# Row maxima of causal attention: the mask added by VectorE inside the maximum, and router logits with stationary weights

## What is computed

```
h = layernorm(x) * (1 + ca) + sa                 # ca, sa, ga ... from silu(c) @ wmod
q, k = [content 16 | rope 64] per head, 16 heads # latent queries 192, latent keys/values 64
attn = softmax(q @ k^T * SCALE + causal mask)    # 512 x 512 per head
x = x + ga * (attn @ v) @ w_out.T
h = layernorm(x) * (1 + cb) + sb
probs = softmax(h @ gate_weight.T)               # 32 experts, the router logits
w_tg = top 8 of probs, normalised, summed by group (8 groups)
act = silu(gate) * up                            # 8 experts chosen beforehand, 96 wide
x = x + gb * sum_g w_tg * (act_g @ down_g)
```

## Time and profile before

| | us |
|---|---|
| median of 3 runs | 1121.26 (1115.88 to 1122.84) |
| profiled execution | 1118.26 |
| its span, first to last instruction | 1116.2 |
| TensorE busy | 1019.5 (91% of the span) |
| VectorE busy | 755.6 (68%) |
| ScalarE busy | 400.0 (36%) |
| GpSimd busy | 420.0 (38%) |

### The profile page before, as it was taken

How to read it: one execution, slowest core, us unless ns; L and a number is a source line. 1 busy time by engine, 2 the same in 40 slices (tenths; PEclk the granted TensorE clock), 3 DMA queues, 4 the chain that set the end, 5 groups by cost and what they waited for, 6 DMA issues and landing times.

```text
span 1116.2 us, 24959 instructions
## 1 busy us (share of the span) xinstructions
PE 1019.5 (91%) x9856; PEld 739.1 (66%) x9856; DVE 755.6 (68%) x1516; ACT 400.0 (36%) x715; POOL 420.0 (38%) x349
## 2 busy tenths in 40 slices
PE   6979989999999999999899999999999998998768
PEld 4556667766776667766676667766677666776456
DVE  6767677675867767586776858577675777757335
ACT  4335432254214533154322542144331553224210
POOL 1627333364316333273333643154332733326100
PEclk9989999999999999999999999999999999999879
DMA  6220000200011000200002000010002000010000
GB/s 187 57 86 2 1 1 1 68 2 2 1 27 43 2 1 1 68 2 1 1 1 69 1 2 1 10 59 2 2 1 68 2 2 1 1 49 2 2 0 19
DMA packets 22232, 23.59 MB, mean 21 GB/s; under 512 B 6314, under 2 KB 20138, under 8 KB 22130
## 3 DMA queue, kind: packets, MB, share of 16 engines
q1 hardware_dynamic: 22130, 22.02, 6.5%
HBM read 17.80 MB, written 4.21 MB: 20 GB/s over the span
## 4 chain that ended last, share of the span: by engine, by line
PE 82%; DVE 9%; issue 4%; ACT 3%; POOL 1%; DMA 1%; DVEq 0%; POOLq 0%; ACTq 0%; SPq 0%
PE ring L1119 17%; PE ring L976 13%; PE ring L977 10%; PE ring L978 10%; PE ring L1190 8%; PE av L1135 6%; PE ring L1099 6%; DVE mcol L858 3%; PE ring L1090 2%; PE ring L1037 2%; PE ring L1107 1%; PE ring L1179 1%; PE av L1148 1%; ACT pt L670 1%; ACT xn L629 1%
## 5 line engine op out<-in xcount | busy, mean ns | idle before, releaser
L670 ACT ACTIVATE pt<-ring 128x384 f32<-128x384 f32 (+1 forms) x384 | 171.0, 533 | 357.5 <-PE ring L1119 315.0
L858 DVE TENSOR_REDUCE mcol<-ring 128x1 f32<-128x128 f32 (+3 forms) x512 | 212.0, 481 | 51.5 <-PE ring L1099 49.5
L560 POOL TENSOR_SCALAR_AFFINE_SELECT pt<-pt 128x512 f32<-128x512 f32 x128 | 83.2, 662 | 345.2 <-ACT pt L670 345.2
L834 DVE TENSOR_TENSOR prod<-ring,table 128x1024 f32<-128x1024 f32 x128 | 156.2, 1221 | 81.4 <-PE ring L978 59.2
L1119 PE MATMUL ring<-rows 32*128 32x512 f32 (+3 forms) x3072 | 165.2, 329 | 25.9 <-DVE mcol L858 15.7
L551 POOL TENSOR_TENSOR rows<-prod,rows 128x1024 fp32r<-128x1024 f32 x64 | 152.4, 2385 | 86.9 <-ACT rows L650 86.9
L1119 PEld LDWEIGHTS ring<-rows 32*128 32x128 f32 x3072 | 118.9, 185 | 74.8 <-issue 41.3
L544 POOL TENSOR_TENSOR prod<-prod 128x512 f32<-128x512 f32 x64 | 84.7, 1324 | 112.3 <-DVE prod L834 112.1
L976 PE MATMUL ring<-h_hi,gu_lo 128*128 128x512 f32 x192 | 80.7, 420 | 14.2 <-DVE h_lo L819 14.2
L1135 PE MATMUL av<-pt,vals 128*17 128x512 f32 (+3 forms) x1024 | 83.7, 440 | 10.1 <-POOL pt L560 10.1
L976 PE MATMUL ring<-h_hi,wq_lo 128*128 128x512 f32 x192 | 84.1, 438 | 1.8 <-DVE wq_lo L780 1.5
(11 more groups left out here) (159 smaller groups left out, 1651.4 us busy)
## 6 DMA issues: line engine op xcount, KB each, us to landing
xn<-x_dram SPq DMA_DIRECT2D x8, 512.0 KB, 4.3
xr<-x_dram SPq DMA_DIRECT2D x8, 512.0 KB, 3.7
out_dram<-xr SPq DMA_DIRECT2D x8, 512.0 KB, 3.2
gate_bc<-gates_scratch SPq DMA_DIRECT2D x8, 256.0 KB, 5.0
pt<-wmod_dram SPq DMA_DIRECT2D x1, 1536.0 KB, 6.4
pt<-gup_t_dram SPq DMA_DIRECT2D x16, 96.0 KB, 2.6
dn<-wu_t_dram SPq DMA_DIRECT2D x1, 640.0 KB, 9.8
xr<-wk_t_dram SPq DMA_DIRECT2D x1, 512.0 KB, 7.9
```

Source lines behind the costliest of these rows:

```text
L670: sc.activation(pt[:, PT_AT[n] + h * w:PT_AT[n] + (h + 1) * w], ps[:, 0:w], ACT.Exp, scale=SCALE).then_inc(exp_ready.sem, 1)
L834: ve.tensor_tensor(prod[:, s % PROD, :, :], ps[:, :].unsqueeze(1).broadcast_to([P, 2, S]), table[:, :, :], ALU.mult).then_inc(rotated.sem, 1)
L858: last = ve.reduce_max(mcol[:, q, h * HR + HD:h * HR + HD + 1], ps[:, at:at + (q + 1) * P], AX_X)
```

## The change

There are three edits, and a new order.

1. The mask matmuls (L1090) go, and with them the bfloat16 identity. The first part's matmul into a bank now has `start=True`. `mask_qk` grows to 512 columns: zero in the first 384, the triangle in the last 128. `reduce` becomes `tensor_tensor_reduce`: it adds a slice of the mask to the row, whose last 128 columns are the diagonal block, takes the maximum into `mcol`, and writes the masked row back to PSUM.
2. `logits` becomes one `three()` with the router weight stationary (32 columns) and 512 tokens moving. The result, experts on partitions, is copied to SBUF by ScalarE (`logits_copy`), transposed back by four small matmuls into the `av` bank (`turn_l`) and copied by VectorE (`turned_l`).
3. Several small tiles move into parts of larger ones.
4. BODY_ORDER and LAST_ORDER are new.

```diff
@@ BODY_ORDER (before)
-load_next.1 loads.0 maxima.010 reduce.010 rope.0200 score.000 rotate.0200 exp.000 rope.0201 rotate.0201 maxima.011
-rope.0210 reduce.011 score.001 clear.000 combine.020 rotate.0210 rope.0211 exp.001 clear.001 maxima.012 value.000
...
-combine.101 qcon.10 exp.031 score.032 qcon_hi.10 value.030 qcon_lo.10 hi.101 exp.032 clear.031 lo.100 value.031
-maxima.100 clear.032 reduce.100 value.032 maxima.101 values.10 attn_out.03 mix.00 reduce.101 mix.01 mixed.00
-rope.1100 values.11 values_out.10 mixed.01 stats2.0 rotate.1100 pow2.0 values_out.11 maxima.102 norm2.0 reduce.102
-rope.1101 rotate.1101 qcon.11 turn2.00 turn2.01 rope.1110 rope.1111 combine.110 modulate2.00 modulate2.01 qcon_hi.11
-low2.00 lo.101 low2.01 up.00 qcon_lo.11 gate.00 rotate.1110 logits.0 tanh.00 gated.00 rotate.1111 gate.01
...
-weighed.00 weighed.01 weigh.04 weigh.05 upped.05 weighed.02 weighed.03 hi.111 weighed.04 weighed.05 down.00 lo.110
-kcon_hi.11 kcon_lo.11 join.00 down.01 join.01 lo.111 store.0
@@ BODY_ORDER (after)
+load_next.1 loads.0 maxima.010 rope.0200 reduce.010 rope.0201 score.000 exp.000 clear.000 rope.0210 rotate.0200
+rotate.0201 score.001 rotate.0210 exp.001 combine.020 maxima.011 value.000 reduce.011 score.002 exp.002 clear.001
+clear.002 value.001 maxima.012 rope.0211 stats1.1 hi.020 reduce.012 qcon.02 rotate.0211 value.002 lo.020 pow1.1
+combine.021 shift.01 kcon.02 qcon_hi.02 shifted.01 qcon_lo.02 rope.0300 rotate.0300 kcon_hi.02 score.010 kcon_lo.02
...
+turn1.11 lo.030 value.011 kcon_lo.03 modulate1.10 value.012 low1.10 hi.031 shift.02 maxima.030 shifted.02 reduce.030
+modulate1.11 score.020 attn_out.01 exp.020 low1.11 lo.031 score.021 clear.020 exp.021 maxima.031 clear.021 value.020
...
+kcon.10 kcon_hi.10 clear.030 value.030 kcon_lo.10 score.032 clear.031 exp.032 kcon.11 rope.1010 rotate.1010
+kcon_hi.11 value.031 clear.032 value.032 combine.100 kcon_lo.11 rope.1011 hi.100 attn_out.03 rotate.1011 qcon.10
+qcon_hi.10 combine.101 mix.00 mix.01 rope.1100 lo.100 qcon_lo.10 qcon.11 qcon_hi.11 mixed.00 mixed.01 values.10
+hi.101 stats2.0 maxima.100 rotate.1100 values_out.10 pow2.0 norm2.0 turn2.00 qcon_lo.11 reduce.100 turn2.01 lo.101
+modulate2.00 rope.1101 rope.1110 rotate.1101 maxima.101 modulate2.01 rope.1111 combine.110 low2.00 low2.01 gate.00
+rotate.1110 tanh.00 logits.0 reduce.101 gate.01 rotate.1111 logits_copy.0 turn_l.0 gated.00 gate.02 tanh.01 tanh.02
+combine.111 turned_l.0 gate.03 gated.01 top.0 gated.02 up.00 ex.0 up.01 gate.04 top2.0 hi.110 up.02 upped.00
...
+upped.04 up.05 upped.05 weigh.05 weighed.04 weighed.05 down.00 maxima.102 reduce.102 join.00 lo.111 down.01 shift.10
+join.01 values.11 shifted.10 values_out.11 store.0
@@ vector, reduce
-                                last = ve.reduce_max(mcol[:, q, h * HR + HD:h * HR + HD + 1], ps[:, at:at + (q + 1) * P], AX_X)
+                                row = ps[:, at:at + (q + 1) * P]
+                                last = ve.tensor_tensor_reduce(row, row, mask_qk[:, (TT - 1 - q) * P:], 1.0, LOWEST, ALU.add, ALU.max,
+                                                               accum_out=mcol[:, q, h * HR + HD:h * HR + HD + 1])
@@ tensor, maxima
-                        for h in range(HG):
-                            pe.matmul(places[h][:, diagonal].rearrange("p (n k) -> p n k", k=P), ident_b[:, :],
-                                      mask_qk[:, :].unsqueeze(1).broadcast_to(own), start=True, stop=False,
-                                      skip_group_check=True)
...
-                                                     k[head, 0:(t + 1) * P], start=False, stop=done, skip_group_check=True)
+                                                     k[head, 0:(t + 1) * P], start=p == 0 and at == 0, stop=done, skip_group_check=True)
@@ tensor, logits
-                        for t in range(TT):
-                            tok = t * P
-                            last = three(ps[:, t * NX:(t + 1) * NX],
-                                         lambda c: h2_hi[:, c, tok:tok + P], lambda c: h2_lo[:, c, tok:tok + P],
-                                         lambda c: gw_hi[:, c, :], lambda c: gw_lo[:, c, :],
-                                         ready=lambda c: wait(pe, lo_ready[1], b, ahead, c) if t == 0 else None)
-                        last.then_inc(full_sem, 1)
+                        three(ps[0:NX, :], *columns(gw_hi, gw_lo, 0, NX), *rows2,
+                              ready=lambda c: wait(pe, lo_ready[1], b, ahead, c)).then_inc(full_sem, 1)
+                    elif kind == "turn_l":
+                        wait_alone(pe, logits_copied, b, ahead, 0)
+                        wait_alone(pe, mix_gated, b, ahead, 0)
+                        for t in range(TT):
+                            last = pe.transpose(av[:, t * NX:(t + 1) * NX], lgT[:, t * P:(t + 1) * P], ident[0:NX, 0:NX])
+                        last.then_inc(logits_turned.sem, 1)
@@ scalar
+                    elif kind == "logits_copy":
+                        ps = wait_full(sc, b, part, ("logits", ahead))
+                        sc.activation(lgT, ps[0:NX, :], ACT.Copy).then_inc(logits_copied.sem, 1)
@@ vector
-                    elif kind == "logits_out":
-                        ps = wait_full(ve, b, part, ("logits", ahead))
-                        ve.tensor_copy(lg, ps[:, 0:TT * NX].rearrange("p (t n) -> p t n", t=TT)).then_inc(logits_read.sem, 1)
+                    elif kind == "turned_l":
+                        wait(ve, logits_turned, b, ahead, 0)
+                        ve.tensor_copy(lg, av[:, 0:TT * NX].rearrange("p (t n) -> p t n", t=TT)).then_inc(logits_read.sem, 1)
```

More of the change, by code:

```diff
@@ L88 @@
-score.012 rope.0310 norm1.1 exp.012 maxima.021 rotate.0310 reduce.021 combine.030 clear.011 clear.012 rope.0311
-kcon.03 maxima.022 rotate.0311 qcon.03 hi.030 value.011 kcon_hi.03 lo.030 qcon_hi.03 combine.031 turn1.10 hi.031
-kcon_lo.03 turn1.11 reduce.022 value.012 qcon_lo.03 shift.02 shifted.02 maxima.030 modulate1.10 reduce.030
-modulate1.11 attn_out.01 score.020 exp.020 low1.10 lo.031 low1.11 score.021 exp.021 clear.020 maxima.031 latent.1
-latent_hi.1 reduce.031 latent_lo.1 maxima.032 value.020 clear.021 reduce.032 value.021 score.022 shift.03 shifted.03
@@ new lines @@
+combine.021 shift.01 kcon.02 qcon_hi.02 shifted.01 qcon_lo.02 rope.0300 rotate.0300 kcon_hi.02 score.010 kcon_lo.02
+rope.0301 exp.010 attn_out.00 clear.010 hi.021 rotate.0301 score.011 norm1.1 exp.011 clear.011 lo.021 value.010
+maxima.020 reduce.020 rope.0310 qcon.03 score.012 qcon_hi.03 rotate.0310 combine.030 qcon_lo.03 rope.0311 exp.012
+rotate.0311 combine.031 clear.012 maxima.021 hi.030 reduce.021 maxima.022 kcon.03 kcon_hi.03 turn1.10 reduce.022
+turn1.11 lo.030 value.011 kcon_lo.03 modulate1.10 value.012 low1.10 hi.031 shift.02 maxima.030 shifted.02 reduce.030
@@ L105 @@
+turn_w.0 tanh.03 gate.05 tanh.04 gated.03 hi.111 wT.0 gated.04 wT_lo.0 lo.110 up.03 upped.01 weigh.00 weigh.01
+upped.02 up.04 weigh.02 upped.03 weigh.03 tanh.05 gated.05 weighed.00 weighed.01 weighed.02 weigh.04 weighed.03
+upped.04 up.05 upped.05 weigh.05 weighed.04 weighed.05 down.00 maxima.102 reduce.102 join.00 lo.111 down.01 shift.10
+join.01 values.11 shifted.10 values_out.11 store.0
 """
 LAST_ORDER = """
[L108 removed]
@@ L119 @@
-modulate2.00 modulate2.01 low2.00 low2.01 up.00 gate.00 logits.0 tanh.00 gated.00 gate.01 logits_out.0 gate.02
-tanh.01 top.0 gated.01 up.01 ex.0 tanh.02 upped.00 gate.03 gate.04 top2.0 turn_w.0 up.02 gated.02 tanh.03 wT.0
-gated.03 gate.05 upped.01 upped.02 tanh.04 tanh.05 gated.04 wT_lo.0 up.03 up.04 weigh.00 upped.03 weigh.01 weigh.02
-gated.05 upped.04 up.05 weigh.03 weighed.00 weighed.01 weigh.04 weigh.05 upped.05 weighed.02 weighed.03 weighed.04
-weighed.05 down.00 join.00 down.01 join.01 store.0
+loads.0 maxima.010 rope.0200 reduce.010 rope.0201 score.000 exp.000 clear.000 rope.0210 rotate.0200 rotate.0201
@@ new lines @@
+score.001 rotate.0210 exp.001 combine.020 maxima.011 value.000 reduce.011 score.002 exp.002 clear.001 clear.002
+value.001 maxima.012 rope.0211 hi.020 reduce.012 qcon.02 rotate.0211 value.002 lo.020 combine.021 shift.01 kcon.02
+qcon_hi.02 shifted.01 qcon_lo.02 rope.0300 rotate.0300 kcon_hi.02 score.010 kcon_lo.02 rope.0301 exp.010 attn_out.00
+clear.010 hi.021 rotate.0301 score.011 exp.011 clear.011 lo.021 value.010 maxima.020 reduce.020 rope.0310 qcon.03
+score.012 qcon_hi.03 rotate.0310 combine.030 qcon_lo.03 rope.0311 exp.012 rotate.0311 combine.031 clear.012
```

90 lines of the change are left out of this document (42 added, 48 removed).

## The result

| | before | after |
|---|---|---|
| median | 1119.99 us | 1166.86 us |
| ratio, 95% interval | | 1.0429, 1.0378 to 1.048: slower |
| span of the profiled execution | 1116.2 | 1166.7 |
| a body | 130.4 | 140.0 |
| mean granted clock of TensorE | 0.983 | 0.956 |

What follows compares the result with a forecast made beforehand. TensorE, busy 91% of the span, was taken as the bound. Masks -3.7, logits -0.76, idle +1.6 and -1.4 gave -4.3 us a body, -34 for eight sequences: median 1085 us, range 1064 to 1110.

Steps and rivals of the forecast that it cites:

- masks: Mask matmuls on TensorE: taking them out saves 0.93 us a group, 3.7 us a body.
- new instruction (idle of the first stretch): From maxima.010 to score.020, banks come back later: 1.6 us a body of new TensorE idle, from 0 to 2.4.
- logits: Router logits on TensorE, 24 matmuls of 2.60 us: the new form saves 0.76 us a sequence, 6.1 in all.
- new order (idle elsewhere): TensorE's holes outside maxima.010 to score.020, 5.5 us: the new order changes them by -1.4 us a body.
- The small tiles that move change no instruction's size: Remark on SP's queue: it stays as before, with no transfer added and no instruction's size changed.
- The walk through the new order: New list with old durations: mix.00's first reader to turn2 takes 8.0 us, leaving a TensorE hole of 2.2.
- Rival (c): Holes at turn2 and of bank waits come to 3 us a body more than counted: 1109 us; chance 0.12.
- 84 ns: VectorE's added cost for each tensor_tensor_reduce to deliver its maximum: 5.4 us a sequence; 0 to 238 ns kept possible.
- (a): Each new instruction adds 238 ns, so VectorE bounds maxima.010 to score.020: 1112 us; chance 0.09.
- (b): New instruction streams at half rate, 536 ns more per 512 columns: 1171 us; chance 0.08, including other costs over 0.27 us.
- The old waits: TensorE's waits of 1.1 us before value.032 and mix.00 go; the 1.5 before gate.00 becomes about 0.7.

Runs made afterwards that it cites:

- newmax: The changed kernel, new order, new logits and loop kept, but with reduce_max and the mask matmuls of the kernel before: 1157.4 us.
- before_unrolled: The kernel before with its loop over the middle six sequences written out, nothing else: 1114.7 us, ratio 0.9947.
- max_only_unrolled: before_unrolled with mask matmuls out and tensor_tensor_reduce in, plus the moved tiles and semaphore increments; logits and order as before: 1109.3 us, ratio 0.9909.
- ttr16_pad: newmax with tensor_tensor_reduce for query tile 0 alone and five more semaphore increments ahead of each reduce: 1198.2 us.
- pad84: The kernel before with seven semaphore increments added ahead of each reduce, loop kept: 1151.9 us.

## Why the prediction was wrong

Term by term, in us for eight sequences, along the ladder above:

| term | forecast | measured |
|---|---|---|
| masks | -29.6 | -12.2 |
| new instruction (idle of the first stretch) | +12.8 | +6.8, by itself 9.1 |
| logits | -6.1 | -6.6 |
| new order (idle elsewhere) | -11.2 | +30.9 |
| loop | 0 | -4.3 + 33.3 = +29.0 |

The order and the loop, 42 and 29 us off, turned a gain into a loss.

**Not in the sum at all: the loop.** "The small tiles that move change no instruction's size", it said, and looked at queues and transfers of data, not at the instructions' own. The accumulator reads, which it had named by the Trainium skill ("VectorE: DVE Perf Modes", Two Vector instructions with no wait between them) and left unpriced, are in the trace as the page has it, 512 of them beside 512 main instructions; in VectorE's loop they are 64 more instructions, 361 where newmax has 297 and keeps its loop. By number alone 361 would still be kept (369 and 370 are), so it is the new instructions, with their reads, that lose it, in a way that stays open. The price is 33.3 us at the jump.

**The walk through the new order.** It took "these durations" from rows of a kernel in which GpSimd rests beside norm2: 8.0 us from mix.00's first reader to `turn2`, a hole of 2.2. In the profile of after those 8.0 are 11.2 (562.61 to 573.83) and the hole is 4.1, since one norm2 instruction takes 2.4 us beside GpSimd (2.0 more) and the two adds of `mixed` take 1.38 and 1.29 us instead of 0.69 (1.3 more). Without the first collision the hole is 1.8, under the 2.2 forecast, but that agreement is partly luck: TensorE there also waits 1.4 us for ScalarE ahead of `maxima.100`, a wait that the walk did not have, and the 8.0 are still 9.0. What the failed step cost is 30.9 us, 21.6 of them shown as `lo.101`, a part of these by the clock. The sum had no term for a clock that falls behind a hole. Rival (c) had the place (`turn2`), but 3 us a body more than counted; 30.9 / 8 = 3.9 lost where 1.4 were to be gained is 5.3 more, and the cause is not in it.

**The masks, -3.7 a body.** The price was right, 3.9 us less of TensorE at the same clock, but it was taken as gained whole. In the old order the run without them gives 12.2 / 8 = 1.5: 1.7 us of waits that the masks had covered come forth, and in most bodies the clock falls behind them. In the new order masks and instruction together give some 20 us where -29.6 + 12.8 = -16.8 was forecast, so there the two terms together held; what they are worth hangs on the order.

**The new instruction.** 84 ns was taken. Start to start, 512 columns take 0.65 us, where four `reduce_max` in 2.48 us with 0.683 for one are (2.48 - 0.683) / 3 = 0.60 apart; busy time of VectorE in a body rises from 91.8 to 95.0 us (before_unrolled, max_only_unrolled), 49 ns for each of 64. Its cost on the path is 6.8 / 8 = 0.85 us a body, increments included, or 9.1 / 8 = 1.1 by itself, against the 1.6 forecast. (That term counted four instructions in each of the seven quads; two of the quads have eight, 3.0 us at most and not 2.4.) Rivals (a) and (b) fall: 50 ns is not 238, and 721 ns for 512 columns is no half rate.

**The logits, -0.76.** Right within what can be told: 6.6 / 8 = 0.8 (the other pair, without the new instruction, gives 9.0 with the clock's part in it). In the profile of after, four of the rows:

```profile
584.18 0.40 PE L988 MATMUL ring<-h_hi,gw_hi 128*32 128x512 f32 x1
584.88 0.40 PE L988 MATMUL ring<-h_hi,gw_hi 128*32 128x512 f32 x1
585.58 0.39 PE L988 MATMUL ring<-h_hi,gu_hi 128*128 128x512 f32 x1
586.61 0.44 PE L1162 MATMUL av<-ident,room 32*128 32x32 f32 x4
```

0.70 for three matmuls and 1.4 for six, as summed. The four transposes last 0.44, but the next matmul starts 0.37 after them (586.98), and it is the 0.37 that compares with the 0.44 of the sum.

**The old waits.** As walked: in the body of after TensorE has no wait before `mix.00`, and 0.4 us are left before the values. New ones ahead of `maxima` (1.7 for `hi`, 1.4 for `exp`) take their place.

## What to carry to other kernels

Before adding instructions to an engine in a loop, count that engine's loop body, accumulator reads included, and look whether the instruction queue's packets in the profile exceed one pass through the program. A wait just behind the jump is the other sign, but the profile calls it "issue" only in some kernels: in ttr16_pad it names a matmul as releaser (`PE ring L991`) for the same wait. Writing the loop out was the cure here. When a list of steps is reordered, check each VectorE instruction with SBUF sources against what GpSimd runs beside it in the new place: durations from the old trace hold only for the old neighbours. Work taken off the engine that bounds the kernel is worth only what no wait stood behind; without the masks it was 12 of 30 us. And when several edits come together, their shares change with what stands beside them: the order costs 30.9 us with the loop written out and 14.2 with the loop.

## What the runs showed of the hardware

- A loop of 394 plain instructions on VectorE is fetched again in each pass (40 packets for 12 to 15), 370 is not; with 48 of the new instructions 345 is. VectorE then stands 2.7 to 8.4 us behind each jump; the same loop moved by 64 instructions went from 6.6 to 2.8.
- `tensor_tensor_reduce` with a PSUM and a bfloat16 source runs 721 ns for 512 columns and adds a 140 ns read of the accumulator that overlaps the next instruction; some 50 ns in all over `reduce_max`.
- Some VectorE instructions whose sources are in SBUF take much longer beside a GpSimd instruction: `tensor_scalar` of 256 columns 2427 ns for 402, ending 0.15 us after GpSimd's; adds of two 512-column tiles 1290 and 1380 for 692.
- A semaphore increment on VectorE costs some 50 ns of the kernel's time (pad84: 33 us for 84 in a body).
- Behind a stretch in which TensorE was busy 1.53 of 5 us the granted clock read 0.53 and 0.78 in the next two.
